# A fused attention and feed-forward layer on one core: when the last projection of the first 512 tokens is run, and in which order the opening's steps stand

## The reference

```
xn  = layernorm(x)
u, v, q, k = split(silu(xn @ W1 + b1))            # 4 x 256 columns, 16 heads of 16
attn = silu(q_h @ k_h^T) / 1024                   # no softmax; per head h
z   = (attn @ v) * u
y   = (layernorm(z) * gamma + beta) @ W2 + b2
h   = gelu((layernorm(xn) * g1 + c1) @ tern(w1)^T + fb1)
out = x + y + (layernorm(h) * g2 + c2) @ tern(w2)^T + fb2
```

## Time and profile before

| | before |
|---|---|
| three runs | 1597.4, 1602.28, 1601.91 us (median 1601.91) |
| the profiled execution | 1597.45 us, its span 1595.7 us |
| mean granted TensorE clock | 0.986 of full |
| TensorE busy | 1482.5 us, 93% of the span |
| ScalarE busy | 1223.6 us, 77% |
| VectorE busy | 896.9 us, 56% |
| silu of the scores (L550) | 983.2 us in 1024 instructions |
| DMA | 123.68 MB, 78 GB/s in the mean |

### The profile page before, as it was taken

The page is one execution under the profiler, slowest core; times in us unless marked ns, Lnnn a source line. Parts: engine busy times, 40 slices in busy tenths (PEclk is TensorE's granted clock), DMA queues, the critical chain, the costliest instruction groups (busy, mean ns, idle before and its releaser), DMA issues.

```text
span 1595.7 us, 27804 instructions
## 1 busy us (share of the span) xinstructions
PE 1482.5 (93%) x9826; PEld 778.7 (49%) x9826; DVE 896.9 (56%) x1716; ACT 1223.6 (77%) x1285; POOL 98.7 (6%) x193
## 2 busy tenths in 40 slices
PE   4799999999999999999999999999999999999986
PEld 3345455454554454544545455545455445554443
DVE  4466734666366653666546674376734666457543
ACT  2578886888868887788877888678886888868883
POOL 2000100001000100001000010000100010000000
PEclk9799999999999999999999999999999999999998
DMA  6561034510444106421165113451044410543100
GB/s 182 112 132 35 20 85 107 127 54 1 108 118 94 54 14 139 113 54 54 41 134 125 38 37 80 107 132 54 1 96 111 113 54 1 127 110 82 27 1 27
DMA packets 62330, 123.68 MB, mean 78 GB/s; under 512 B 7664, under 2 KB 9328, under 8 KB 61168
## 3 DMA queue, kind: packets, MB, share of 16 engines
q1 hardware_dynamic: 62192, 121.81, 32.4%
HBM read 79.84 MB, written 41.94 MB: 76 GB/s over the span
## 4 chain that ended last, share of the span: by engine, by line
issue 93%; POOLq 6%; POOL 1%; DVE 0%; DVEq 0%
POOLq L517 3%; POOLq L509 1%; POOLq L493 1%; POOL rs L503 1%; POOLq L502 0%; POOLq L511 0%; POOLq L507 0%; POOLq L505 0%; POOLq L519 0%; POOLq L522 0%; POOLq L203 0%; POOL rs L494 0%; DVE part L764 0%; DVEq L203 0%; POOLq L536 0%
## 5 line engine op out<-in xcount | busy, mean ns | idle before, releaser
L550 ACT ACTIVATE attn<-scores 128x1024 f32<-128x1024 f32 x1024 | 983.2, 1025 | 260.6 <-PE scores L920 259.7
L939 PE MATMUL outs<-attn,V 128*32 128x512 f32 x4096 | 501.0, 607 | 0.0
L920 PE MATMUL scores<-QS,KS 64*128 64x512 f32 x2048 | 407.9, 461 | 74.8 <-ACT attn L550 51.9
L920 PEld LDWEIGHTS scores<-QS,KS 64*128 64x128 f32 x2048 | 165.3, 186 | 390.6 <-ACT attn L550 314.6
L939 PEld LDWEIGHTS outs<-attn,V 128*32 128x32 f32 x4096 | 108.0, 110 | 240.8 <-issue 240.7
L793 DVE SCALAR_TENSOR_TENSOR hid<-fill,ratq,fb1b 128x512 f32<-128x512 f32 x128 | 96.2, 751 | 75.3 <-PE fill L994 70.0
L810 DVE TENSOR_TENSOR tmp<-fill,l2g 128x512 f32<-128x512 f32 x128 | 88.5, 692 | 88.8 <-PE fill L1003 77.5
L1010 PE MATMUL fill<-Wq,hgh 128*128 128x256 f32 x512 | 130.6, 293 | 0.0
L976 PE MATMUL fill<-xp,W1h 128*128 128x512 f32 x384 | 125.5, 408 | 2.3 <-DVE xp L834 1.5
L1010 PE MATMUL fill<-Wq,hgl 128*128 128x256 f32 x512 | 124.9, 282 | 0.0
L1010 PEld LDWEIGHTS fill<-Wq,hgh 128*128 128x128 f32 x512 | 97.3, 190 | 18.0 <-issue 10.4
(11 more groups left out here) (110 smaller groups left out, 1415.1 us busy)
## 6 DMA issues: line engine op xcount, KB each, us to landing
QS<-q_scratch SPq DMA_DIRECT2D x128, 256.0 KB, 7.2
k_scratch<-kst SPq DMA_DIRECT2D x64, 256.0 KB
q_scratch<-qst SPq DMA_DIRECT2D x64, 256.0 KB
KS<-k_scratch SPq DMA_DIRECT2D x64, 256.0 KB, 4.1
KS<-k_scratch SPq DMA_DIRECT2D x128, 128.0 KB, 5.0
xin<-in_x SPq DMA_DIRECT2D x8, 1024.0 KB, 6.2
out_dram<-part SPq DMA_DIRECT2D x16, 512.0 KB, 2.6
w1raw<-in_W SPq DMA_DIRECT2D x1, 1024.0 KB, 7.0
```

The lines of the kernel that those rows point to most:

```text
L550: nc.scalar.activation(attn_of(g)[:, 2 * hf:2 * hf + 2, :], SP[:, 2 * hf:2 * hf + 2, :], ACT.Silu).then_inc(s_silu, 1)
L920: ins = mm(SP[:, j, :], KS[rows, pair, t * P:(t + 1) * P], QS[rows, pair - c * PPC, h * HALF:(h + 1) * HALF], start=True, stop=True)
L939: ins = mm(OP[32 * j:32 * j + 32, g // RUN % 2, :], V[:, t, c * HPC // 2 + j, o * DH:o * DH + 2 * DH], attn_of(g)[:, n, :], start=(o == 0 ...
```

## The change

All 64 rows of `TABLE` are new. The output steps `zt`, `zs`, `a` of pairs 2 and 3 (tokens 512 to 1023) still stand at the start of the next batch; those of pairs 0 and 1 now stand in rows 50 to 63 of the same batch, where z of these tokens is complete after group 47. `late` marks the ones that stay behind, and the semaphore values, the first and last batch and the end (`EPI`) follow it. `zX` is now used by pair 2 alone. Each half of `part` is stored on its own: the first half's store stands in SyncE's program between the reading back of k.0.1 and of q.0.1. The opening has an order of its own: the low part of W1 is made ahead of `xn.0`, k and q of both halves stand ahead of all v, and SyncE reads k of batch 0's first channel half back without waiting for the writes of q.

The diff (lines of the table left out; its rounds stand above):

```diff
 SLOTS = [[(n.split(".")[0], *map(int, n.split(".")[1:])) for n in row.split()] for row in TABLE]
 assert len(SLOTS) == GROUPS
 
 POST = ("zt", "zs", "a")
+def late(s):
+    return s[0] in POST and s[1] >= NP // 2
 
 
 def is_next(s):
@@ -137,8 +142,8 @@
 ORDER = [s for g in range(GROUPS) for s in SLOTS[g]]
 PIECES = [s for s in ORDER if s[0] in FILLERS]
 POS = {s: n for n, s in enumerate(PIECES)}
-NPOST = sum(s[0] in POST for s in PIECES)
-assert all(POS[s] < NPOST for s in PIECES if s[0] in POST) and NPOST % 2 == 0
+NPOST = sum(late(s) for s in PIECES)
+assert all(POS[s] < NPOST for s in PIECES if late(s)) and NPOST % 2 == 0
 
 
 def in_order(*steps):
@@ -148,8 +153,10 @@
 
 
 
-in_order("a.0", "zs.2")
-in_order("a.1", "zs.3")
+in_order("f1.7.1", "zs.0", "a.0", "zs.1", "a.1")
+in_order("f2.3", "a.1")
+in_order("a.2", "g.0.0")
+assert not {("zs", 0), ("zs", 1), ("zt", 0), ("zt", 1)} & {s for g in range(GROUPS - RUN) for s in SLOTS[g]}
 in_order("a.3", "y.0", "f1.1.1", "y.3")
 in_order("a.3", "px", "y.1", "ln1")
 in_order("px", "y.2", "f1.5.1", "ln1", "xn.0")
@@ -168,6 +175,11 @@
 Y_ORDER = [s[1] for s in ORDER if s[0] == "y"]
 
 
+PRO = [(n.split(".")[0], *map(int, n.split(".")[1:])) for n in (
+    "ln1 xn.0 xn.1 xt.0 xn.2 xt.1 k.0.0 q.0.0 xn.3 xt.2 xt.3 k.0.1 q.0.1 v.0 v.1 v.2 v.3 vs.0").split()]
+assert sorted(PRO) == sorted(s for s in ORDER if is_next(s) or s == ("vs", 0))
 def bank_of(step):
     return POS[step] % 2
 
@@ -184,8 +196,8 @@
 
     k = bank_of(step)
     if isinstance(body, int) and body < 0:
-        return pieces_of(k, is_next, step)
-    base = body * pieces_of(k) + pieces_of(k, is_next) - pieces_of(k, lambda s: s[0] in POST)
+        return sum(s in POS and bank_of(s) == k for s in PRO[:PRO.index(step) + 1])
+    base = body * pieces_of(k) + pieces_of(k, is_next) - pieces_of(k, late)
     if isinstance(body, int) and body == NB:
         base = base - pieces_of(k, is_next)
     if isinstance(body, int) and body == NB - 1:
@@ -357,7 +369,7 @@
 
         def z_of(i):
 
-            return zX if i % 2 else yT
+            return zX if i == NP // 2 else yT
 
         def hid_of(t):
 
@@ -369,12 +381,11 @@
 
         def steps(g, first, last):
             for s in SLOTS[g]:
-                if first and s[0] in POST or last and (is_next(s) or s == ("vs", 0)):
+                if first and late(s) or last and (is_next(s) or s == ("vs", 0)):
                     continue
                 yield s
 
-        PRO = [s for s in ORDER if is_next(s) or s == ("vs", 0)]
-        EPI = [s for s in ORDER if s[0] in POST]
+        EPI = [s for s in ORDER if late(s)]
 
         def last_filler(bank):
 
@@ -405,7 +416,9 @@
 
                 written = 4 * WROTE * b + WROTE * (NH * c + h + 1)
                 sp.wait_ge(s_kw, written)
-                sp.wait_ge(s_qw, written)
+                if not (isinstance(b, int) and b == 0 and c == 0):
+                    sp.wait_ge(s_qw, written)
                 pairs = slice(c * PPC, (c + 1) * PPC)
                 cols = slice(h * HALF, (h + 1) * HALF)
                 kv = kd[c].rearrange("(e w) r n -> e r w n", e=2)
@@ -427,16 +440,15 @@
                         sp.dma_start(QS[e * TERMS + at_row:e * TERMS + at_row + QROWS, :, cols].bitcast(F32),
                                      qv[e, :, :, cols]).then_inc(s_qst[h], 16)
 
-            def store(b):
-                for i in range(2):
-                    wait_evacuated(sp, b + 1, ("a", 2 * i + 1))
-                    ts = slice(i * T // 2, (i + 1) * T // 2)
-                    sp.dma_start(ov[b, :, ts, :], part[:, ts, :]).then_inc(s_out, 16)
+            def store(b, i):
+                wait_evacuated(sp, b + i, ("a", 2 * i + 1))
+                ts = slice(i * T // 2, (i + 1) * T // 2)
+                sp.dma_start(ov[b, :, ts, :], part[:, ts, :]).then_inc(s_out, 16)
 
             def body(b, first=False, last=False):
                 if not first:
-                    store(b - 1)
+                    store(b - 1, 1)
                 for h in range(NH):
                     write_parts(b, 1, h, not first)
                     if first and h == 0:
@@ -452,7 +464,11 @@
                     for h in range(NH):
                         write_parts(b + 1, 0, h, True)
                         load_k(b + 1, 0, h)
+                        if h == NH - 1:
+                            store(b, 0)
                         load_q(b + 1, 0, h, True)
+                else:
+                    store(b, 0)
 
 
             load_x(0)
@@ -469,12 +485,13 @@
             for h in range(NH):
                 write_parts(0, 0, h, False)
                 load_k(0, 0, h)
+                sp.wait_ge(s_qw, WROTE * (h + 1))
                 load_q(0, 0, h, False)
             body(0, first=True)
             with sp.Fori(1, NB - 1) as b:
                 body(b)
             body(NB - 1, last=True)
-            store(NB - 1)
+            store(NB - 1, 1)
             sp.wait_ge(s_out, 32 * NB)
 
 
@@ -516,7 +533,7 @@
                 if kind in ("zt", "ln2", "ln1"):
                     pool.drain()
                 if kind == "zt":
-                    pool.wait_ge(s_mv3, NP * (b - 1) + a[0] + 1)
+                    pool.wait_ge(s_mv3, NP * (b - late((kind, *a))) + a[0] + 1)
                     rsqrt(rs3[:, 2 * a[0]:2 * a[0] + 2], mv3[:, 2 * a[0]:2 * a[0] + 2, 1], rp3[:, :], 2, s_rs3)
                 elif kind == "ln2":
                     pool.wait_ge(s_mv2, NP * b + a[0] + 1)
@@ -758,7 +775,7 @@
                 elif kind == "a":
                     i = a[0]
                     wait_filled(dve, b, me)
-                    dve.wait_ge(s_rs3, NP * (b - 1) + i + 1)
+                    dve.wait_ge(s_rs3, NP * (b - late(me)) + i + 1)
                     for j in range(2):
                         t = 2 * i + j
                         ins = V_.scalar_tensor_tensor(out=part[:, t, :], in0=FP[:, k, j * D:(j + 1) * D],
@@ -879,12 +896,12 @@
             V_.memset(ones[:, :], 1.0).then_inc(s_ones, 1)
             step(-1, "ln1")
             split_w1(False)
+            dve.drain()
+            split_w1(True)
             dve.wait_ge(s_b1, 32)
             for s in PRO:
                 if s != ("ln1",):
                     step(-1, *s)
-                if s == ("xn", 0):
-                    split_w1(True)
             body(0, first=True)
             with dve.Fori(1, NB - 1) as b:
                 body(b)
@@ -1013,13 +1030,13 @@
                     i = a[0]
                     if i % (NP // 2) == 0:
 
-                        pe.wait_ge(s_z, DC * NH * b - (i < NP // 2))
+                        pe.wait_ge(s_z, DC * NH * b + (0 if late(me) else 3))
                     for j in range(2):
                         for c in range(DC):
                             toks = slice((2 * i + j) * P, (2 * i + j + 1) * P)
                             ins = nc.tensor.transpose(bank[:, j * D + c * P:j * D + (c + 1) * P], uz[:, c, toks], ident[:, :])
                 elif kind == "a":
-                    pe.wait_ge(s_zs, NP * (b - 1) + a[0] + 1)
+                    pe.wait_ge(s_zs, NP * (b - late(me)) + a[0] + 1)
                     passes = [(w, part, c) for c in range(DC) for w, part in ((W2h, 0), (W2h, 1), (W2l, 0))]
                     for j in range(2):
                         for n, (w, part, c) in enumerate(passes):
```

116 lines of the change are left out of this document (58 added, 58 removed).

## The result

The changed kernel took 1611.56 us (median of 5 runs, 1610.25 to 1617.77), the kernel before 1601.91 beside it (5 runs): ratio 1.008, 95% interval 1.005 to 1.0109, so 0.8% slower. The forecast was 1610. The profiled execution took 1610.25 (span 1608.5, mean granted clock 0.984) against 1597.45, so the sum of +8.7 stands against +12.8 between the two profiled executions and +9.7 between the medians. The total is nearly right, but several of its terms are not, as the next table shows.

What follows compares the result with a forecast made beforehand. TensorE is busy nearly throughout, yet single waits decide; a round costs its fillers plus about 3.25. Terms summed to +8.7 on the profiled 1597.45, so 1606, and 1610 for the median, 4.5 above; range 1587 to 1626.

Steps and rivals of the forecast that it cites:

- The opening: Before the first scores: k.0.0 starts 2.85 earlier, k is read back sooner, first scores at 42.8 instead of 47.93; -5.1 us.
- Batch 0: First batch: two zt and two a added, +4.1; its new waits +1.6; the 1.30 wait at 61.44 goes, -1.3.
- The inner batches: Six middle batches: all work is the same, only what waits differs; +2.4 us each.
- q.1.1: Inner batch: ScalarE waits 2.0 to 2.2 until q.1.0's write has landed and frees `qst`; +1.1 a batch.
- Start of a batch: Inner batch's start: zt.2 waits 0.3 for z, zs.2 stands behind zt.3's statistics on VectorE; +0.8 a batch.
- xn.1: Inner batch: ln2.3's statistics, 2.47, now stand ahead of xn.1 on VectorE; +0.3 a batch.
- round 25: Inner batch: VectorE has 5.6 of work against 5.7 in one round, zt.1 waits for zt.0's bank; +0.2 a batch.
- gains nothing: Round 7, a gelu round: taking f1.2.1 out wins no time; the gelu rounds and empty round sum to 0.
- The clock: Rival: half-rate TensorE stretches at 48 to 58 and in batches 1 and 7 may go; -9 together, 1601; chance 0.12.
- Last batch: Final batch: zt and a of pairs 0 and 1 move from full to nearly empty rounds; -1.0 with the waits.
- tail: After the last z: two pairs to finish instead of four, 11.5 to the last a instead of 15.5; -4.0.
- The likeliest case: The forecast itself: summed terms of +8.7 make the changed kernel slower, 1610 us; chance 0.50.

Runs made afterwards that it cites:

- the experiment: The kernel before with the changed kernel's opening alone (order of steps, W1's low part, no wait for q's write): 1597.08 us, ratio 0.9986.
- written-out pair: The kernel before and the changed one, each with its batch loop written out on all engines instead of a hardware loop: 1602.54 us and 1578.29 us.

## Why the prediction came out as it did

- **The opening, -5.1 forecast, -1.7 measured (-2.2 in the experiment, -4.6 to +0.2).** The step that failed is "VectorE's chain of xt.1 gives back the rest, and k.0.0 starts near 18.35". W1's low part, priced at 0.5, made xn.0 2.05 later (14.12 instead of 12.07), because the subtraction blocks GpSimd's power and not only VectorE; and xn.2, which the new order puts ahead of xt.1's split, was held until 20.1 by the clearing of V, a GpSimd instruction that the prediction leaves out. The second binds: with the low part back behind xn.0, k.0.0 started no earlier. So k.0.0's gain of 2.85 became 0.15, k's write came 0.14 earlier and q's 1.2 (27.43 against 28.63). The wait of 1.30 at batch 0's round 2 shrank to 0.55 instead of going.
- **Batch 0, +4.4 (4.1 + 1.6 - 1.3), measured +4.7.** Right in size.
- **The inner batches, +14.4 forecast, +15.9 measured.** Near, but not by the forecast's parts, as the next four points say.
- **q.1.1, forecast +1.1.** The mechanism and the place were right: the wait was forecast at 2.0 to 2.2 and measured at 2.2 to 2.6, round 5 grew by 0.8, and taking the wait away gave 1.74 a batch.
- **Start of a batch, forecast +0.8.** This is the step whose mechanism failed most. I priced z with 0.3 and let VectorE's jump cost nothing, though the kernel before showed 4.82 idle at that place and I read it as a wait for products only. The price was 1.35 to 2.25 at TensorE, and VectorE's statistics in front of zs.2, my other half of it, cost TensorE at most 0.2. But the same step also missed a gain: written out, the new plan's start is 5.5 shorter than the old one's (20.7 against 26.2). Some 1.7 of that is work that was moved away (zt.0, zt.1, and f2.7 against v.3), 2.6 on average is the wait for K; the stretch at half the clock behind that wait, in which the products took 3.64, is the likely rest. In the loop the five starts with a jump came out at 123.7 against 126.3, and the two without one fell by 5.3 and 6.6.
- **Late rounds, forecast +0.3 for xn.1 and +0.2 for round 25.** xn.1 cost nothing (round 22 is 5.30 before and after). Rounds 21 to 30 grew by 2.8 in an inner batch, and in the written-out pair by nearly as much (+17.4 in eight batches), but they took in 3.2 of fillers, so by the prediction's own rule (a round costs its fillers plus 3.25) this is the moved work and no new wait. 0.5 of the 2.8 is the loop's gaps on VectorE in round 26.
- **Where the moved work gave nothing back.** Rounds 3 to 8 lost 2.0 of fillers and became no shorter: q.1.1's 0.8 is one reason, and round 7 is the other, 9.94 and 9.93 with f1.2.1 gone, which the prediction had said ("gains nothing"). Rounds 15 to 20 cost another 1.0 with 0.6 more of fillers, against a forecast of 0; round 14, emptier by g.3.0, gives back 0.6 of it.
- **The clock.** The rival had the stretches that it named half right: the one of 48 to 58 now ended at 54.6, and those at the starts of batches 1 and 7 went, with three more at the starts of batches 4 to 6. Nothing was won by it in all, for new ones came: at the starts of batches 2 and 3 (at 634.9, where zt.2 waits for z), and in rounds 6 to 8 of four batches; the mean granted clock went from 0.986 to 0.984. The row of 253 to 259, which the prediction read as a fall with TensorE busy, lies behind TensorE's wait of 2.53 for K that ended at 253.34: the clock was at 0.50 from 252.8 on.
- **Last batch, -1.0 forecast, -2.4 measured; tail, -4.0 and -3.6.** Two pairs instead of four behind the last z: right, at 12.4 from the last z to the last a where 11.5 was forecast.

So +8.7 came out near +12.8 partly by luck: the opening missed 3.4, the last batch and the tail 1.0 the other way, and inside the inner batches the jump that I left out was set off by K's wait that I left out too. The likeliest case was the right side for a reason that I named only in half: q.1.1's wait held, the batch start's did not. What the looped change really is: a better plan, by 24 us when nothing jumps (1578.29 against 1602.54), whose gain the jump (20.2 at the starts, with the half-rate stretches there), the gaps on VectorE and half-rate stretches elsewhere give back and more.

## What to carry to other kernels

When a plan moves the last work of a loop body, look on each engine for the idle time between its last instruction before the jump and its first after it, put down to anything at all: the jump lies inside, and is free only while another wait is as long. Where a plan moves an engine's last instruction towards the jump and puts what hangs on that engine at the top of the body, the jump shows. Here neither moving the top's work one round down nor moving the last work one round up helped; writing that engine's loop out did. And price a moved VectorE instruction with two SBUF inputs against what GpSimd does in those microseconds. Removing one wait may also hand its time to the clock, so a gain measured in one form of a kernel isn't to be added to another's.
